# Attention in a macaron layer: the causal mask of query tiles 2 and 3 moves from TensorE products into VectorE's search for the maxima

## The reference, cut to what matters

```python
q, k, v = (proj(W_q), proj(W_k), proj(W_v))
scores = jnp.einsum('bhqd,bhkd->bhqk', q, k) / jnp.sqrt(jnp.float32(DK))
causal = jnp.tril(jnp.ones((s, s), dtype=bool))
scores = jnp.where(causal, scores, NEG)
attn = jax.nn.softmax(scores, axis=-1)
out = jnp.einsum('bhqk,bhkd->bhqd', attn, v)
```

## Time and profile before

| | us |
|---|---|
| time, median of 3 runs | 1513.49 |
| lowest and highest run | 1510.73, 1516.84 |
| span of the profiled execution, first to last instruction | 1510.3 |
| first feed-forward, to the first score | 563 |
| attention, 563 to 993 | 430 |
| second feed-forward, from 993 | 517 |
| TensorE busy over the span | 1445.4 (96%) |
| VectorE busy over the span | 957.4 (63%) |
| ScalarE, GpSimd busy | 668.7, 586.1 |

### The profile page before, as it was taken

One profiled execution on the slowest core, in us unless ns is written; L12 is line 12 of the kernel. 1 busy time (PEld: TensorE's weight loads), 2 busy tenths in 40 slices (PEclk: granted clock), 3 DMA queues, 4 the chain that ended last, 5 costly groups with the idle time before them and its releaser, 6 DMA issues. The chain is left out here.

```text
span 1510.3 us, 28902 instructions
## 1 busy us (share of the span) xinstructions
PE 1445.4 (96%) x8968; PEld 1163.4 (77%) x8968; DVE 957.4 (63%) x2013; ACT 668.7 (44%) x1347; POOL 586.1 (39%) x832
## 2 busy tenths in 40 slices
PE   5999999999989969999999999989999999999998
PEld 2688888888878756667666666658888788888887
DVE  5679765556545657677676776535786455555566
ACT  4534453434433535665565665543322234333332
POOL 6538810333323023464465354321288333333100
PEclk9999999999999978999999999969999999999999
DMA  9988998443485935454645444445464634356941
GB/s 347 343 309 308 322 379 323 141 140 110 150 304 178 341 87 141 100 127 121 146 125 120 124 122 123 152 132 206 182 238 150 226 103 147 105 183 218 306 132 57
DMA packets 176534, 285.82 MB, mean 189 GB/s; under 512 B 20738, under 2 KB 125698, under 8 KB 176146
## 3 DMA queue, kind: packets, MB, share of 16 engines
q1 hardware_dynamic: 134642, 206.31, 43.3%
q0 software_dynamic: 19104, 56.64, 10.3%
q10 hardware_dynamic: 22656, 21.11, 4.9%
HBM read 144.20 MB, written 109.84 MB: 168 GB/s over the span
## 5 line engine op out<-in xcount | busy, mean ns | idle before, releaser
L1709 PE MATMUL f_bank<-f_xparts,f_sw 128*128 128x512 f32 x1536 | 375.1, 394 | 2.3 <-DVEq L1639 2.3
L1709 PEld LDWEIGHTS f_bank<-f_xparts,f_sw 128*128 128x128 f32 x1536 | 282.7, 190 | 57.2 <-DVEq L1639 3.3
L1160 POOL DMA_INDIRECT outputs_by_choice<-f_yr,f_home x160 | 153.4, 959 | 359.3 <-DVE f_yr L1663 292.8
L2428 DVE TENSOR_REDUCE at_mx<-at_ps 128x1 f32<-128x384 f32 (+3 forms) x352 | 213.9, 632 | 107.7 <-PE at_ps L2558 107.4
L2319 ACT ACTIVATE at_pT<-at_ps 128x512 f32<-128x512 f32 (+1 forms) x352 | 194.3, 559 | 73.1 <-PE at_ps L2574 64.7
L2247 POOL TENSOR_SCALAR_AFFINE_SELECT at_pT<-at_pT 128x128 f32<-128x128 f32 (+2 forms) x352 | 123.4, 358 | 219.0 <-ACT at_pT L2319 214.5
L1118 POOL DMA_INDIRECT rows_by_slot<-f_xq,slot x128 | 146.3, 1143 | 123.9 <-issue 72.4
L2574 PE MATMUL at_ps<-fa_qT,fa_kT 98*128 98x256 f32 (+3 forms) x512 | 173.4, 392 | 5.9 <-DMA fa_qT<-at_mT 4.0
L1652 DVE TENSOR_TENSOR f_sil<-f_sil,f_bank 128x256 f32<-128x256 f32 x160 | 67.4, 421 | 164.1 <-ACT f_sil L1294 162.3
L1274 ACT CAST f_hparts<-f_hid 128x512 fp32r<-128x512 f32 x128 | 79.4, 620 | 201.1 <-DVE f_hid L1545 201.0
L1545 DVE TENSOR_TENSOR f_hid<-f_sil,f_bank 128x512 f32<-128x512 f32 x128 | 87.8, 686 | 121.3 <-PE f_bank L1709 107.9
(11 more groups left out here) (261 smaller groups left out, 2479.6 us busy)
## 6 DMA issues: line engine op xcount, KB each, us to landing
f_ring<-weights_in_parts SPq DMA_DIRECT2D x32, 768.0 KB, 5.7
weights_in_parts<-fa_whi SPq DMA_DIRECT2D x30, 768.0 KB, 7.8
f_rawx<-rows_by_slot ACTq DMA_DIRECT2D x152, 128.0 KB, 2.1
at_whi<-weights_in_parts SPq DMA_DIRECT2D x16, 768.0 KB, 8.3
fa_ew<-in_L_ffn_routed_w_dram SPq DMA_DIRECT2D x42, 256.0 KB, 4.9
rows_by_slot<-zero POOLq DMA_DIRECT2D x10, 1024.0 KB, 23.1
f_xq<-xn_rows POOLq DMA_DIRECT2D x32, 256.0 KB, 4.7
fa_ew<-outputs_by_choice SPq DMA_DIRECT2D x8, 1024.0 KB, 9.2
```

The costliest lines, as they stand in the source:

```text
L1160: nc.gpsimd.indirect_dma_start(dram.yk, bass.IndirectOffsetOnAxis(ap=home[:, i:i + 1], axis=0), yr[:, i % 4, :], None).then_inc(y_st[i % 4 ...
L1709: ins = pe.matmul(ps[j % 2][:, :], sw12[:, wp, k, w, j * P:(j + 1) * P], xparts[:, u, xp, k, :], start=(i == 0), stop=(i == 3 * KD - 1))
L2428: v.tensor_reduce(own, ps1[i % RING1][:, 0:heads * w].rearrange("p (j a x) -> p j a x", a=min(heads, 2), x=w), AX.X, ALU.max).then_inc(mx_ ...
```

## The change

For the one-head units of `score1` (units 3 to 10, query tiles 2 and 3) the mask product is left out. VectorE instead runs `tensor_tensor_reduce`, which reads the scores from PSUM and a bf16 mask from SBUF, adds the two, writes the sum as bf16 to a buffer that nobody reads, and puts the maximum of the sums into `mx`. The mask for it is a wider tile `maskz`: three blocks of zeros ahead of the four triangles, so that one slice gives zeros for the earlier key tiles and the triangle for the last. The three unread buffers lie in tiles that are idle in the attention (`zero`, and the raw projection weights `wraw`). Units 0 to 2 keep their mask product and their tensor_reduce.

```diff
-    r.maskq = m.sb("maskq", [P, GROUP, P], BF16)
+    r.maskz = m.sb("maskz", [P, CT - 1 + GROUP, P], BF16)
...
-                nc.gpsimd.memset(maskq[:], 0.0).then_inc(mask_made, 1)
+                nc.gpsimd.memset(maskz[:], 0.0).then_inc(mask_made, 1)
...
+        maskq = maskz[:, CT - 1:, :]
+        late_mask = maskz[:].rearrange("p b x -> p (b x)")
+        spare = att.wraw[:].rearrange("p k i n -> p (k i n)")
+        masked = [a.bitcast(BF16) for a in (g.zero[:], spare[:, 4 * D:5 * D], spare[:, 5 * D:6 * D])]
...
                 dve.wait_ge(s1_done, i + 1)
+                if heads == 1:
+
+                    at = (h % 2 * 2 + h // 2) * CT + qi
+                    v.tensor_tensor_reduce(masked[i % RING1][:, 0:w], ps1[i % RING1][:, 0:w],
+                                           late_mask[:, (CT - 1 - qi) * P:CHUNK], 1.0, -3.0e38, ALU.add, ALU.max,
+                                           mx[:, G % 2, at:at + 1]).then_inc(mx_done, 1)
+                    return
...
-                    pe.matmul(ps[:, j * w:(j + each) * w], qT[0:ROWS, G % KEEP, (h + j) // 2, qi * P:w],
-                              kT[0:ROWS, G % KEEP, h + j:h + j + each, 0:w], start=(j == 0), stop=False,
-                              skip_group_check=True)
+                    ins = pe.matmul(ps[:, j * w:(j + each) * w], qT[0:ROWS, G % KEEP, (h + j) // 2, qi * P:w],
+                                    kT[0:ROWS, G % KEEP, h + j:h + j + each, 0:w], start=(j == 0), stop=(heads == 1),
+                                    skip_group_check=True)
+                if heads == 1:
+
+                    ins.then_inc(s1_done, 1)
+                    return
```

More of the change, by code:

```diff
@@ L496, in attention_rows @@
     r.pT = m.sb("pT", [P, len(UNITS1) + 4, CHUNK])
-    used = 4096 + 1024 + 2 * 128 + 512 + 1024 + 512 + 3 * 1024 + 80 + 5 * 1024 + 64 + 256 + 2 * 256 + 15 * CHUNK
+    used = 4096 + 1024 + 2 * 128 + 512 + 1024 + 512 + 3 * 1024 + 80 + 5 * 1024 + 64 + 448 + 2 * 256 + 15 * CHUNK
     m.sb("rest", [P, n - used])
     return r
-FREE = 16016
+FREE = 16208
 UNITS1 = [(0, 0, 4), (1, 0, 2), (1, 2, 2)] + [(t, h, 1) for t in (2, 3) for h in range(GROUP)]
@@ L1164, in _ @@
             if not exact:
-                identb, maskq = pre.identb, pre.maskq
+                identb, maskz = pre.identb, pre.maskz
                 nc.gpsimd.memset(identb[:], 0.0).then_inc(mask_made, 1)
@@ L1170, in _ @@
                                         base=0, pattern=[[-1, P]], channel_multiplier=1).then_inc(mask_made, 1)
-                nc.gpsimd.memset(maskq[:], 0.0).then_inc(mask_made, 1)
+                nc.gpsimd.memset(maskz[:], 0.0).then_inc(mask_made, 1)
                 pool.wait_ge(mask_made, 3)
-                nc.gpsimd.affine_select(out=maskq[:], in_=maskq[:], compare_op=ALU.is_ge, fill=MASK,
+                nc.gpsimd.affine_select(out=maskz[:, CT - 1:], in_=maskz[:, CT - 1:], compare_op=ALU.is_ge, fill=MASK,
                                         base=0, pattern=[[0, GROUP], [-1, P]], channel_multiplier=1)
@@ L2020, in attention @@
         stat, mv, veps, rstd = mine.stat, mine.mv, mine.veps, mine.rstd
-        wo, identb, maskq, pick, hiT, loT = mine.wo, mine.identb, mine.maskq, mine.pick, mine.hiT, mine.loT
+        wo, identb, maskz, pick, hiT, loT = mine.wo, mine.identb, mine.maskz, mine.pick, mine.hiT, mine.loT
+        maskq = maskz[:, CT - 1:, :]
+        late_mask = maskz[:].rearrange("p b x -> p (b x)")
+        spare = att.wraw[:].rearrange("p k i n -> p (k i n)")
+        masked = [a.bitcast(BF16) for a in (g.zero[:], spare[:, 4 * D:5 * D], spare[:, 5 * D:6 * D])]
         va, mx, mT, pT, oT, av = mine.va, mine.mx, mine.mT, mine.pT, mine.oT, mine.av
@@ L2725, in macaron_kernel @@
                 pre.att = att
-                pre.identb, pre.maskq = ahead.identb, ahead.maskq
+                pre.identb, pre.maskz = ahead.identb, ahead.maskz
                 norm_first(nc, z, g, dram, pre, x_flat)
@@ L2729, in macaron_kernel @@
             post.rows = attention_rows(z, Mem(nc, both, "at_"))
-            post.rows.identb, post.rows.maskq = ahead.identb, ahead.maskq
+            post.rows.identb, post.rows.maskz = ahead.identb, ahead.maskz
             post.tail = attention(nc, z, g, dram, att, post.rows, post.own, pre)
```

## The result

The changed kernel takes 1503.99 us (median of 5 runs, 1502.69 to 1511.53), beside 1513.67 us for the kernel before on the same chip (5 runs). The ratio is 0.9926, 95% interval 0.9902 to 0.995: 0.74% faster, some 11 us (the two medians differ by 9.7). The forecast was 1497 us.

A forecast was written before the change was run, and what follows sets the result against it. TensorE's stream was taken to bound the attention, except where three chains of VectorE and DMAs hold it. 32.0 us gross less 16.1 lost took 15.9 off the 1510.3 span; with 3.2 for the median, 1497 us, range 1481 to 1513.

The forecast's parts named there:

- The mask's price: TensorE time saved per removed mask product: 0.144 us beside two 512-column products, 0.08 in step 5, mean 0.125.
- The stream's price: VectorE's streaming instruction was taken as equal to the reduction it replaces, 687 ns for 512 columns.
- The term d = 0.12: VectorE's added one-column write behind each of 256 streams: 0.12 us each, 31 us in all.
- Rival (c): VectorE's stream needs two cycles for an element, so the kernel gets 24 us slower, 1537 us; chance 0.15.
- (b): Rival: VectorE's two instructions cost 0.3 to 0.4 us more than the reduction, nothing measurable left, 1506 to 1513; chance 0.15.
- Three chains in a regular batch: Attention stretches not running through the masks, where TensorE's saving is lost: together 2.305 us a batch, seven batches, 16.1 us.
- The first chain: Kind 2 into kind 3: VectorE and DMA set 7.5 us, six masks gain nothing; loss 0.99 us a batch.
- The third chain: Kind 0 into kind 1: SyncE's DMAs, reciprocal and `shift` hold score2; ten masks, 0.43 us slack, loss 0.82 a batch.
- the second chain: Kind 0: `project` waits for `shift` to free its bank, VectorE sets it from step 10; loss 0.495 us a batch.
- the waits forecast for TensorE: Sign: TensorE waits for the maxima's DMA in kinds 1 and 3, and for `mx_done`, well above the few us before.
- The step that failed: Chain losses were counted for seven batches, the first being taken to have no such side work: 16.1 us.
- nothing here makes TensorE idle for long, so I leave it there: TensorE's clock, at its upper level (1.00) in the windows read, was assumed to stay there.

The follow-up runs named there:

- Experiment 2: Changed kernel with no mask products and the plain reduction in one-head units, their maxima unmasked: 1506.53 us, ratio 0.993 to the kernel before.
- experiment 4: Changed kernel with the reciprocal moved from step 1 to step 2 on VectorE, behind `shift`: 1490.73 us, ratio 0.9829 to the kernel before.
- 3: Changed kernel with no mask product in any unit and plain reductions over unmasked scores: 1508.0 us, ratio 0.9948 to the kernel before.
- experiment 1: Changed kernel with mask products kept on TensorE in every unit, the mask added twice in one-head units: 1520.07 us, ratio 1.0016 to the kernel before.
- 6: Kernel before, all mask products in place, with the reciprocal moved to step 2 behind `shift`: 1508.88 us, ratio 0.9952 to the kernel before.
- experiment 5: Changed kernel with the reciprocal and its sending moved to step 4 and its fetching to step 6: 1551.53 us, ratio 1.0231 to the kernel before.
- 8: Changed kernel with the reciprocal behind `shift` and `shift` ahead of the maxima of its step: 1486.31 us, ratio 0.9792 to the kernel before.

## Why the prediction was right, and where it was not

The direction was right, and so was the main mechanism, that chains of VectorE, SyncE's queue and a DMA hold back part of what TensorE saves. The time lay 7 us above the forecast, inside its range. Step by step:

**The mask's price.** 0.144 in a step of two 512-column products was right (0.60 to 0.46). In step 5 I put 0.08; it was 0.11. Taking 0.13 for the mean, the gross is 256 x 0.13 = 33 us in place of 32.0.

**VectorE's two instructions.** The stream's price was right. The term d = 0.12 was too large: the accumulator's read overlaps the stream's end and the next operation's start, so 0.01 to 0.04 is what the engine loses. Experiment 2 against the change shows no cost in time. Rival (c) is refuted by the 688 ns. Of (b), the result "nothing measurable" is refuted; its fixed cost of each instruction isn't there. The Trainium skill, "VectorE: DVE Perf Modes", section "Two Vector instructions with no wait between them", says that an operation with an accumulator output is two instructions. The trace agrees, and adds the price.

**Three chains in a regular batch.** I forecast 4.0 gross less 2.305, so 1.70 a batch. Batches 1 to 6 gained 1.58, 1.42, 1.09, 2.76, 2.57 and 0.98, on average 1.73. The size was right, but by some luck: with 0.13 for a mask and 0.02 for d the same sum gives 4.16 - 2.10, some 2.1 a batch (an estimate), so the d that was too large made up for a chain that held more than I had said. The first chain behaved as said: in the changed kernel step 9 of kind 2 starts at 812.50 and the first score2 of kind 3 at 819.97, 7.47 us, against 7.50. The third chain was put at a loss of 0.82 for having slack of 0.43, and there I looked at the wrong end of it. The slack was measured at the first score2 of kind 1, which in rounds 5 to 25 of the changed kernel waits for no DMA. What waits for `shift` is `project` of kind 1, whose weight loads start as soon as `shift` (841.45 + 0.26) has freed the bank:

```profile
841.76 1.23 PEld L2614 LDWEIGHTS at_psX<-fa_xnT,fa_wqk 128*128 128x128 f32 x6 [0.48 <-DVE at_mT L2448]
```

In the kernel before, `project` already stood only 0.05 to 0.2 us behind `shift` in these rounds, so there was next to no slack. The chain is the one from `shift` to `shift` of experiment 4, and kind 0 lost all of its 1.04. That also covers the second chain, which is the same chain's beginning, and whose 0.495 I had counted beside it. Of the waits forecast for TensorE, that on the maxima's DMA came in kind 3, and in kind 1 only in round 29 (4.0 to 7.5 us in all); that on `mx_done` grew from 1.3 to 3.2 us (products' rows). One that isn't among the signs that I named, on the bank for `project`, grew from 2.5 to 7.8. VectorE's busy time was to rise by 20 to 35 us and rose by 7.5: 20.7 us of records came, but they overlap their neighbours.

**The step that failed** is "The first batch has no such side work yet, so I count seven", and with it that the last one is regular. Unsaid, it also took SyncE's queue to run alike in both kernels, from one stretch (836.28 to 843.95) in which one issue took 1.26 us. I gave these two batches 4.0 + 1.70 = 5.7 us; their cells hold 0.58 - 2.10 = -1.5. (Eight of their masks, those of group 0, lie ahead of the first cell, where the time from the first score to the first product that turns the maxima fell by 0.3 us.) These 7 us are nearly the whole miss.

In the first batch the reciprocal of round 3 waits as later ones do. It starts 2.42 us after the product that turns the maxima, where it was 1.15 before, and the round of kind 2 ahead of it is 0.81 longer. One of its eleven issues took 1.61 us, the slow one shown above; in the kernel before none there took more than 0.62. Experiments 2 and 3 have one there too (1.3 us each), and lose 0.5 us in that round.

In the last batch, round 29, one of the eleven issues takes 1.48 us in place of 0.6 (in the kernel before one was as slow there), the chain was late already, and the reciprocal waits 2.6 us, the longest of the wait row above, where it waited 1.9 before. TensorE then waits twice:

```profile
944.95 0.45 PE L2565 MATMUL at_ps<-fa_kT,fa_qT 96*128 96x384 f32 x1 [1.47 <-DVE at_mx L2439]
...
947.17 0.80 PE L2589 MATMUL at_ps<-fa_qT,fa_kT 98*128 98x512 f32 x1 [1.12 <-DMA fa_qT<-at_mT]
```

and as the second wait begins its granted clock falls to the lower level, 1.2 GHz, as the windows show (columns as in the earlier trace rows):

```profile
945.00:947.00 2.00, 1.05 (x6) 0.79 (x6) 1.99 (x9) 0.60 (x1) 0.41 (x1) 0.83 0.02 4
947.00:949.00 2.00, 1.83 (x6) 1.60 (x7) 0.00 (x0) 0.74 (x2) 0.46 (x2) 0.50 0.04 8
949.00:951.00 2.00, 2.00 (x8) 0.86 (x10) 1.40 (x4) 1.48 (x3) 0.35 (x2) 0.50 0.62 192
951.00:953.00 2.00, 2.00 (x16) 0.59 (x12) 0.00 (x0) 0.16 (x1) 0.29 (x1) 0.50 0.96 304
```

In the kernel before, with waits of 0.52 and 0.90 us at the same two places, the same stage has 1.00:

```profile
954.00:956.00 2.00, 1.10 (x9) 0.79 (x7) 1.16 (x3) 0.73 (x2) 0.63 (x1) 1.00 0.06 12
956.00:958.00 2.00, 2.00 (x17) 1.01 (x19) 1.29 (x2) 2.00 (x4) 0.58 (x2) 1.00 0.18 51
```

It is tempting to say that a shorter stream makes TensorE idle more and so costs clock, and I had written "nothing here makes TensorE idle for long, so I leave it there". But the runs don't show that. In experiment 1, which keeps every mask product, the clock falls in the same stage of its profiled execution, behind waits of which one is shorter than in the kernel before and the other as long:

```profile
963.05 0.44 PE L2565 MATMUL at_ps<-fa_kT,fa_qT 96*128 96x384 f32 x1 [0.17 <-DVE at_mx L2439]
...
965.23 0.69 PE L2585 MATMUL at_ps<-fa_qT,fa_kT 98*128 98x512 f32 x1 [0.92 <-DMA fa_qT<-at_mT]
```

```profile
965.50:967.50 2.00, 2.00 (x8) 1.51 (x8) 0.13 (x1) 1.19 (x2) 0.29 (x1) 0.50 0.08 16
```

Its reciprocal was not late (1.37 us after the product that turns the maxima, 1.73 before), and still its round 29 is 1.6 us longer than before, with some 3 us at the lower level. That leaves little but the clock to explain it. In the changed kernel round 29 is 2.65 us longer than the regular 12.45 of its kind, with some 7 us at the lower level, which at half speed cost at most 3.5 (an estimate). Most of that loss may be clock, and the clock's fall isn't shown to come from the change. Another fall, about 902 to 905 us, lies in the kind 2 round of batch 6 (-0.17, where 0.78 is normal), which is 0.95 us longer than the regular 14.28 and holds a slow issue as well. The mean clock of a whole execution is 0.97 to 0.98 in the runs of both kernels. From 600 to 957 us it is 1.00 in the kernel before and in experiment 4, and 0.98 in the changed kernel. All of this is one profiled execution for each kernel.

**Outside the rounds** the attention began 2.9 us later and what follows the last round took 3.2 less. The first score stands at 563.2 us before, at 566.1 here, at 566.0 to 567.4 in experiments 2 to 4 and at 566.5 in 6, which has the old mask tile, so the delay is not the change's work.

## What to carry to other kernels

When work leaves the busiest engine, look for chains that go from an event to its next occurrence without that work, and measure that distance (here `shift` to `shift`): a round whose chain doesn't hold the removed work gives back nothing, however busy the engine looks. To find a chain's slack, look at everything that waits for its end; here I took the score2 products, and `project` was waiting. An instruction that waits for a transfer must not stand ahead of one that the next stage waits for, if it is not itself needed first; here moving a reciprocal of 0.54 us by one step was worth 7 us before the change and about 15 after it, while moving it two steps further cost some 60 (experiment 5, where its own reader waited). Before a single stage's loss is put down to an edit, see whether a kernel without that edit shows it too, as with the clock in round 29. The version to use does all of the work, with `shift` and reciprocal as in experiment 4 (1490.73 us) or 8 (1486.31 us): 1.7 to 2.1% less than before, and 1.0 to 1.4% less than the changed kernel.

## What the runs showed of the hardware

- An add and a running maximum over one PSUM and one bf16 SBUF source takes 688 ns for 512 columns, like the plain reduction, and the read of its accumulator (81 ns by its record) lets the next operation start with it, or at most 0.03 us behind it.
- A bf16 product of 128 columns between fp32 products of 512 costs 0.14 us, two and a half times its columns at the measured rate.
- Waits of TensorE of 1.5 and 1.1 us, with 1.1 us of products between them, went with some 7 us at half clock from about the start of the second. Waits of 0.5 and 0.9 us at the same places of the kernel before left the clock at 1.00, and waits of 0.2 and 0.9 us in experiment 1 went with some 3 us at half clock. So the length of the waits alone doesn't tell whether the clock falls.
- An 8 KB transfer was usable about 1.6 to 2.4 us after the end of its issue on SyncE's queue, and 2.3 to 3.3 us after it on ScalarE's, while SyncE issued others, measured to the start of the reciprocal that waited for it. Each issue holds SyncE's queue for about 0.6 us, but one in some thirty for 1.0 to 2.1 us.
